# Cross attention of a decoder layer: score terms of a head pair stacked by DMA into one product of 100 rows, all engines' work in a group in a new order, and two implied waits left out

## The chip, the cores and the metric

The kernel runs on one core of one Trainium2 chip. The metric is the device time of one execution in microseconds (us). TensorE (PE) multiplies, VectorE (DVE), ScalarE (ACT) and GpSimd (POOL) compute elementwise, SyncE (SP) issues most DMAs. Each engine works through its own instructions in their order and waits on semaphores.

## The reference

Four sequences of 1024 tokens, width 256, 77 context rows each. Three blocks are added to x in turn, each behind a layer norm: a recurrent block (shift, projections, a scan), cross attention over the context, and a mixture of 16 experts (top 2).

```python
x = x + attn(layernorm(x))                 # scan over time, 64 states
q = (layernorm(x) @ wq.T + bq)             # 16 heads of 16
k, v = ctx @ wk.T + bk, ctx @ wv.T + bv    # 77 keys
x = x + softmax(q k^T / 4) v @ wo.T + bo
x = x + moe(layernorm(x))                  # top 2 of 16 experts, 256 wide, gated
```

## The kernel before

The work has three stages. The first does the recurrent block for all 4096 tokens, then `s1_turn`. The second is the cross attention with the router of the experts, in 8 groups of 512 tokens (`GROUPS`; two groups share a sequence b). The third, the experts, takes 79 blocks of 128 rows that the router has scattered to `xs_rows` in memory.

A group passes through three phases that run one group apart. Phase 1 of group g+1: norm by ScalarE (`norm_q`, L685), turn by TensorE (`s1_turn`, L970) and copy (`evac_t`, L696), query products (`s1_q`, L977), the fp16 high half QH by ScalarE (`evac_q`, L703) and the low half QL by VectorE (`s1_ql`, L1386), then an estimate of each head's score maximum: 16 products `s1_max` (L985) into two banks, each reduced by VectorE (L1396), negated into high and low halves (`s1_mh`, L1400), turned (`s1_mt`, L1000) and copied to MT (`evac_m`, L709). Phase 2 of group g: for each half m of the heads (8 heads), 616 key columns in 5 chunks of 128 (the last 104). `s2_scores` (L1006) adds four products into a bank: minus the maxima over an indicator matrix IND (32 rows), then high keys by low queries, low keys by high queries and high by high, where the keys stand block by block, masked per head, in KCUR (`kcur`, L495, by POOL). Two banks alternate; ScalarE takes the exponential of each chunk into PB (`exps`, L715). Then `s2_pv` (L1026) makes numerator and denominator in fp32, by products of 32 columns each, with VCUR (`vcur`, L1271, by VectorE from memory) and a mask MV. `s2_attn` (L1408) divides. PB, NUM and DEN are single, so the exponentials of one half wait for the value product of the other. Phase 2 of group g-1 ends with the out projection (`s2_out`, L1046), the residual add (`s2_x2`, L1414) and the norm before the experts (`root3`, `norm_3`, `rows_hi`, `low_rows`, `s3_turn`). Phase 3 of group g-2: logits (`s3_logits`), top 2, prefix sums (`s3_prefix`, L1072), slots (`s3_slots`, L1465) and 8 scatters by POOL (L542). The banks of the logits and prefix sums are those of the maxima, so the maximum products wait for the run counts (`run_s`).

The order within a group is written out by hand in a function `body` for each engine (TensorE's at L1078, ScalarE's at L750, VectorE's at L1491, POOL's at L553), called in a loop over b for the middle groups. In TensorE's body: 5 chunks of m=0, logits, out projection, turn, prefix, value product m=0, query products, 5 chunks of m=1 with the 16 maximum products between their products, value product m=1, turn of the maxima, `s3_turn`. Beside this the 48 pieces of expert weights are loaded by SP (`wload`, L320), scaled and rounded by ScalarE (`whi`, L613) and their low halves made by POOL (`split`, L487): 6 pieces before the groups, 6 in each of the first 7 groups. At the end POOL scatters the last group, SP and ScalarE write padding rows (`pads`, L300), and TensorE starts the experts' products when all 48 pieces are split (L1138).

## Time and profile before

| | us |
|---|---|
| median of 3 runs (769.19 to 773.58) | 772.86 |
| the profiled execution | 767.49 |
| its span, first to last instruction | 765.7 |
| TensorE, VectorE, POOL, ScalarE busy | 613.7, 488.7, 351.0, 328.9 |
| mean granted TensorE clock | 0.898 |

"Busy" is the time in which at least one instruction of that engine runs. A granted clock of 1.00 is 2.4 GHz and of 0.50 is 1.2 GHz. In rows of the timeline the columns are start, length, engine, line, operation, output and inputs, number of instructions merged, and in brackets the idle time before and what ended it.

### The profile page before, as it was taken

The page shows a single profiled execution, that of the slowest core. Times are in us where ns is not written, and L with a number is a line of the kernel's source. Part 1 is how long each engine was busy: PE and PEld are TensorE (multiplying, and loading weights), DVE is VectorE, ACT ScalarE, POOL GpSimd, SP SyncE. Part 2 cuts the span into 40 slices and gives each one's busy share as a digit, 9 for nine tenths or more (in the row PEclk, how much of TensorE's full clock was granted, in tenths as well). Part 3 has the DMA queues.
Part 4 walks back from the last instruction along what each step waited for, and adds up shares of the span by engine and source line. Part 5 has one row for each costly group of instructions (what it writes and reads, how often), then busy time and mean ns, then how long its engine had stood idle before and what let it go on. Part 6 is the DMA issues. An engine that isn't in the chain of part 4 may idle for free.

```text
span 765.7 us, 13490 instructions
## 1 busy us (share of the span) xinstructions
PE 613.7 (80%) x3148; PEld 314.6 (41%) x3149; DVE 488.7 (64%) x1381; ACT 328.9 (43%) x739; POOL 351.0 (46%) x433
## 2 busy tenths in 40 slices
PE   1987888778999797979798973069999999999910
PEld 0666333523434252525252543034555555555510
DVE  5576325756487566866767644446777777777796
ACT  3854634226666464655555332013333333333331
POOL 5864623232744656467557355412333333333353
PEclk9998987679999899989899985579999999999975
DMA  9811000074000101010101011523333333333397
GB/s 321 272 11 12 0 1 0 2 270 146 1 1 12 49 2 56 4 55 0 55 1 57 1 55 56 168 55 84 91 87 88 85 87 88 86 86 88 73 377 275
DMA packets 93219, 62.37 MB, mean 81 GB/s; under 512 B 68186, under 2 KB 78558, under 8 KB 93056
## 3 DMA queue, kind: packets, MB, share of 16 engines
q1 hardware_dynamic: 85168, 44.04, 20.8%
q0 software_dynamic: 6864, 16.86, 6.5%
q10 hardware_dynamic: 1152, 1.06, 0.5%
q8 instruction: 15, 0.25, 0.1%
q14 instruction: 20, 0.16, 0.1%
HBM read 27.97 MB, written 25.56 MB: 70 GB/s over the span
## 4 chain that ended last, share of the span: by engine, by line
PE 51%; SPq 14%; DVE 12%; issue 9%; ACT 6%; DMA 4%; POOL 2%; another core or an unknown queue 1%; ACTq 0%; POOLq 0%; DVEq 0%
SPq L379 7%; PE bank L1037 5%; PE bank L891 4%; PE bank L866 4%; PE bank L995 3%; PE bank L1017 3%; SPq L380 3%; PE bank L855 3%; PE bank L1054 3%; PE bank L1019 3%; SPq L375 3%; PE bank L1068 2%; PE bank L1160 2%; PE bank L1161 2%; PE bank L1163 2%
## 5 line engine op out<-in xcount | busy, mean ns | idle before, releaser
L588 POOL DMA_INDIRECT y_rows<-AR x79 | 77.2, 977 | 165.4 <-ACT AR L815 161.1
L491 POOL TENSOR_TENSOR W<-STG,W 128x512 f16<-128x512 f32 (+1 forms) x48 | 56.1, 1169 | 122.2 <-ACT W L620 120.9
L804 ACT ACTIVATE AR<-AR 128x256 f32<-128x256 f32 x79 | 32.9, 417 | 160.4 <-DVE AR L1585 138.1
L1410 DVE RECIPROCAL AR<-bank 128x512 f32<-128x512 f32 x16 | 53.7, 3354 | 38.1 <-PE bank L1037 31.2
L548 POOL DMA_INDIRECT xs_rows<-AR,SLOT x64 | 63.4, 991 | 27.4 <-issue 18.1
L720 ACT ACTIVATE AR<-bank 128x512 f32<-128x512 f32 (+1 forms) x80 | 47.6, 596 | 51.9 <-PE bank L1023 47.9
L1396 DVE TENSOR_REDUCE MX<-bank 128x4 f32<-128x308 f32 x128 | 56.6, 475 | 18.4 <-PE bank L995 13.8
L1585 DVE TENSOR_SCALAR AR<-bank 128x256 f32<-128x256 f32 x79 | 33.5, 424 | 51.5 <-PE bank L1163 47.9
L1160 PE MATMUL bank<-W,AR 128*128 x158 | 61.3, 388 | 0.0
L1161 PE MATMUL bank<-W,AR 128*128 x158 | 61.1, 387 | 0.0
L995 PE MATMUL bank<-KCUR,AR 128*128 (+1 forms) x128 | 41.9, 329 | 19.4 <-DVE MX L1396 10.0
L1601 DVE TENSOR_TENSOR AR<-bank,AR 128x256 f16<-128x256 f32 x79 | 33.5, 425 | 24.1 <-ACT AR L808 20.2
L1163 PE MATMUL bank<-W,AR 128*128 x158 | 47.9, 385 | 0.0
L1158 PE MATMUL bank<-BEX,AR 128*128 128x512 f16 x79 | 30.9, 391 | 20.2 <-DMA AR<-xs_rows 18.2
L1181 PE MATMUL bank<-W,AR 128*128 x158 | 40.7, 277 | 0.0
L1182 PE MATMUL bank<-W,AR 128*128 x158 | 40.6, 277 | 0.0
L1037 PE MATMUL bank<-AR,VCUR 128*32 128x512 f32 (+1 forms) x256 | 35.8, 682 | 4.3 <-ACT AR L720 4.3
L815 ACT ACTIVATE AR<-bank 128x256 f32<-128x256 f32 x79 | 30.1, 381 | 15.5 <-PE bank L1184 13.5
L1172 PE MATMUL bank<-ID,AR 128*128 128x128 f32 x158 | 32.3, 286 | 4.8 <-issue 2.8
L1596 DVE SCALAR_TENSOR_TENSOR AR<-AR 128x256 f32<-128x256 f32 x79 | 33.6, 425 | 2.7
L995 PEld LDWEIGHTS bank<-KCUR,AR 128*128 128x128 f16 x128 | 12.4, 98 | 52.6 <-DVE MX L1396 28.8
L620 ACT ACTIVATE W<-STG 128x512 f16<-128x512 f32 (+1 forms) x48 | 30.2, 630 | 8.2 <-ACT STG L618 5.0
(229 smaller groups left out, 1443.6 us busy)
## 6 DMA issues: line engine op xcount, KB each, us to landing
W<-in_wexp SPq DMA_DIRECT2D x16, 768.0 KB, 5.3
W<-y_rows SPq DMA_DIRECT2D x8, 1024.0 KB, 15.3
X<-in_x SPq DMA_DIRECT2D x4, 1024.0 KB, 11.9
out<-X SPq DMA_DIRECT2D x8, 512.0 KB, 8.1
CST<-in_cst SPq DMA_DIRECT2D x1, 1309.0 KB, 8.4
AR<-xs_rows SPq DMA_TRANSPOSE x79
AR<-xs_rows SPq DMA_DIRECT2D x79, 1.0 KB
y_rows<-AR POOLq DMA_INDIRECT x79
```

What stands on the lines that cost most here:

```text
L379: sp.dma_start_transpose(XTS[:, q], xs_halves[ds(row, P), 0:2 * D]).then_inc(XTIN[q], 16)
L491: pool.tensor_tensor(w[:, 1], STG[:, q], w[:, 0], ALU.subtract).then_inc(s["w_split"], 1)
L548: pool.indirect_dma_start(xs_rows, bass.IndirectOffsetOnAxis(ap=SLOT[:, par, k, j:j + 1], axis=0), RB[:, par, j, :], None, bounds_check=XS ...
L588: pool.indirect_dma_start(y_rows, bass.IndirectOffsetOnAxis(ap=NIX[:, k:k + 1], axis=0), CY[:, k, :], None, bounds_check=TOPK * NTOK - 1, ...
L720: act.activation(PB[0:rows, c, :], SC[(m * NCH + c) % 2][0:rows, :], ACT.Exp)\
L995: pe.matmul(MXB[:, half, 0:GK // 2], QH[:, par, m, j * P:(j + 1) * P], KCUR[:, ds(bp, 1), m, 0, 4 * half:4 * half + 4].rearrange("p a h k ...
L1037: mm = pe.matmul(o[32 * j:32 * j + 32, :], w[0:rows, j + v, v].rearrange("p a e -> p (a e)"), PB[0:rows, j + v, :], start=(v == 0), stop=( ...
L1160: pe.matmul(GUP[q], XTS[:, k, c], w_at(e, c * 2 * PW + LOW, F), start=False, stop=False)
L1161: pe.matmul(GUP[q], XTS[:, k, c], w_at(e, c * 2 * PW, F), start=False, stop=False)
L1163: mm = pe.matmul(GUP[q], XTS[:, k, 2 + c], w_at(e, c * 2 * PW, F), start=False, stop=(c == DC - 1))
L1396: dve.tensor_reduce(MX[:, j, m * HG + 4 * half:m * HG + 4 * half + 4], MXB[:, half, 0:GK // 2].rearrange("p (h k) -> p h k", k=KEYS), AX.X ...
L1410: dve.reciprocal(AT[:, m], DEN[:, :]).then_inc(s["rec_s"], 1)
```

## The change

**Keys and queries.** For each pair of heads, KS holds a block of 100 rows: high, low and again high halves of 32 rows of keys, and 4 rows of a pattern of ones that picks the minus maxima of its heads. QS holds the matching rows of the queries: high, high, low, and four rows of maxima. One product over 100 rows gives the sum of all four terms. Four chunks of an m are now 64 keys of two heads (128 columns); the fifth holds the other 13 keys of all eight heads, each pair in 32 columns, by four narrow products. QS is filled in every group through memory: QH and QL are written to `q_rows` and read back in 6 DMAs, MT is written to `m_rows` and read back in 2, all issued by SP (`q_stack`). QH and QL are single now, so `evac_q` waits for their writes. KS is filled once, before the first group, from masked copies KM that POOL makes. KCUR keeps only the high half. V is copied once into VP and VR, so `vcur` and the trip through `v_flat` go, as does IND.

**Order.** All four bodies are rewritten, TensorE's loop over groups is written out, and the pieces of weights are now 12 before the groups, 3 in each of the 8, 6 before the last scatter and 6 behind it; the last two experts are loaded after all value products.

**Two waits.** `c_gu` no longer waits for `cu_r`, nor `c_tg` for `cgl_r`; both are implied by other waits.

```diff
@@ SP, once @@
+            sp.wait_ge(s["km_r"], 1)
+            kv_in(KS[3 * 32:QROWS].rearrange("p n b k -> p (n b) k"),
+                  PAT[3 * 32:QROWS].unsqueeze(1).broadcast_to([QROWS - 3 * 32, PAIRS * B, PKW]))
+            for m in range(DC):
+                for i in range(GT):
+                    for t, v in enumerate((0, 1, 0)):
+                        kv_in(KS[32 * t:32 * t + 32, m * GT + i].rearrange("p b k -> p (b k)"),
+                              KM[32 * i:32 * i + 32, v, m].rearrange("p b k -> p (b k)"))
...
@@ SP, each group @@
+            def q_stack(g):
+                first = g == 0
                 for m in range(DC):
+                    sp.wait_ge(s["ql_r"], 2 * g + (m + 1))
+                    if not first:
+                        sp.wait_ge(QSIN[m], g * QS_IN)
+                    for v, q in enumerate((QH, QL)):
+                        sp.dma_start(q_rows[m, v], q[:, m]).then_inc(QOUT[m], 16)
                 for m in range(DC):
+                    sp.wait_ge(QOUT[m], 32 * g + 32)
+                    if not first:
+                        sp.wait_ge(s["sc_mm"], g * (2 * NCH) - (1 - m) * NCH)
+                    for t, v in enumerate((0, 0, 1)):
+                        sp.dma_start(QS[32 * t:32 * t + 32, m], q_in[m, v]).then_inc(QSIN[m], 16)
+                sp.wait_ge(s["mT_r"], g + 1)
+                sp.dma_start(m_rows, MT[:, :]).then_inc(s["m_out"], 16)
+                sp.wait_ge(s["m_out"], 16 * g + 16)
+                for m in range(DC):
+                    sp.dma_start(QS[3 * 32:QROWS, m], m_in[m]).then_inc(QSIN[m], 16)
+            for g in range(GROUPS):
+                q_stack(g)
+                wload(g + (A_EXP + 2))
@@ POOL @@
+            for n in range(A_PIECES // 2):
+                split(n, n % 2)
+            pool.wait_ge(s["a_kv"], 4)
+            pool.memset(CST[:, 0:B * DC * P], 0.0).then_inc(s["vr_z"], 1)
+            for n in range(A_PIECES // 2, A_PIECES):
                 split(n, n % 2)
...
             def body(g, b, par, out=True, log=True, attn=True, nxt=True, nextk=None):
                 if attn:
+                    for k in range(PIECES):
+                        split(g * PIECES + (A_PIECES + k), (par + k) % 2)
                     add_bo(g)
...
+            for n in range(B_PIECES, C_HALF):
+                split(n, n % 2)
             scatter(GROUPS - 1, 1)
+            for n in range(C_HALF, NPIECE):
+                split(n, n % 2)
@@ ScalarE body @@
                 if attn:
+                    for k in range(PIECES):
+                        whi(g * PIECES + (A_PIECES + k), (par + k) % 2, g * 16 + 16 * (A_EXP + 1))
+                if nxt:
+                    for j in range(GT):
+                        norm_q(g + 1, j)
+                if attn:
+                    exps(g, 0, 0, first)
+                    exps(g, 0, 1, first)
                 if log:
                     pair_exp(g - 2)
...
                 if nxt:
                     evac_t(g + 1)
...
+                if attn:
+                    exps(g, 0, 2, first)
+                if nxt:
+                    evac_q(g + 1, 0)
+                if attn:
+                    exps(g, 0, 3, first)
+                if nxt:
+                    evac_q(g + 1, 1)
+                if attn:
+                    exps(g, 0, 4, first)
                 if out:
                     norm_3(g - 1)
                     rows_hi(g - 1, 1 - par, b - 1 + par)
@@ TensorE @@
+                o = SC[(m * NCH + c) % 2]
+                if c < GT:
+                    mm = pe.matmul(o[:, :], KS[0:QROWS, m * GT + c, b, 0:P], QS[0:QROWS, m, c], start=True, stop=True)
+                else:
+                    for i in range(GT):
+                        mm = pe.matmul(o[32 * i:32 * i + 32, :], KS[0:QROWS, m * GT + i, b, P:PKW],
+                                       QS[0:QROWS, m, i], start=True, stop=True)
+                mm.then_inc(s["sc_mm"], 1)
...
                 if out:
                     s2_out(g - 1)
+                if attn:
+                    s2_scores(g, b, 0, 0)
+                    s2_scores(g, b, 0, 1)
                 if nxt:
                     s1_turn(g + 1)
+                if attn:
+                    s2_scores(g, b, 0, 2)
+                if nxt:
+                    s1_q(g + 1, 0)
+                if attn:
+                    s2_scores(g, b, 0, 3)
+                if nxt:
+                    s1_q(g + 1, 1)
+                if attn:
+                    s2_scores(g, b, 0, 4)
                 if log:
                     s3_prefix(g - 2)
...
                     units = s1_max(g + 1, 1 - par, b1, bp1) if nxt else iter(())
+                    for _ in range(2):
+                        next(units, None)
+                    s2_pv(g, b, 0, units)
                     for c in range(NCH):
+                        s2_scores(g, b, 1, c)
+                        for _ in range(1):
+                            next(units, None)
                     s2_pv(g, b, 1, units)
+                    for _ in units:
+                        pass
...
-                if not isinstance(n, int) or n >= 2:
-                    pe.wait_ge(s["cu_r"], n - 1)
                 pe.wait_ge(XTIN[k], 16 * (t + 1))
...
                 pe.wait_ge(s["cgd_r"], n + 1)
-                if not isinstance(n, int) or n >= 2:
-                    pe.wait_ge(s["cgl_r"], n - 1)
@@ VectorE body @@
                 if log:
                     s3_slots(g - 2, par)
+                if nxt:
+                    s1_ql(g + 1, 1 - par)
+                    s1_max(g + 1, 0, 5)
                 if attn:
                     s2_attn(g, 0)
                 if nxt:
-                    s1_ql(g + 1, 1 - par)
-                    s1_max(g + 1)
+                    s1_max(g + 1, 5, 16)
                     s1_mh(g + 1)
```

In `s2_pv` a maximum product is taken after each quarter but the last: three in each value product.

## Rows read from the trace of the kernel before

**Rows 1.** Windows by stage: length; busy PE, PEld, DVE, ACT, POOL; clock, DMA, GB/s.

```profile
147.00:503.00 356.00, 282.66 (x1461) 127.12 (x1460) 221.28 (x614) 169.32 (x328) 185.50 (x224) 0.88 0.17 54
503.00:731.00 228.00, 217.32 (x1253) 120.62 (x1253) 162.89 (x474) 80.10 (x235) 74.64 (x77) 0.98 0.37 88
```

**Rows 2.** The same view, one group of the loops.

```profile
359.90:400.10 40.20, 35.25 (x189) 15.38 (x187) 27.13 (x73) 22.69 (x45) 22.13 (x27) 0.92 0.08 27
```

**Rows 3.** Timeline of TensorE: starts of value products of groups 1, 2, 6, 7.

```profile
206.42 1.06 PE L1037 MATMUL bank<-AR,VCUR 128*32 128x512 f32 x8
222.66 0.64 PE L1037 MATMUL bank<-AR,VCUR 128*32 128x512 f32 x4 [0.52 <-ACT AR L720]
240.44 1.06 PE L1037 MATMUL bank<-AR,VCUR 128*32 128x512 f32 x8
...
400.07 1.50 PE L1037 MATMUL bank<-AR,VCUR 128*32 128x512 f32 x12
433.30 1.93 PE L1037 MATMUL bank<-AR,VCUR 128*32 128x512 f32 x16
```

**Rows 4.** Timeline, TensorE: a score chunk's first and last product, and the next chunk's first.

```profile
347.14 0.38 PE L1017 MATMUL bank<-MT,IND 32*128 32x512 f16 x1
...
347.90 0.38 PE L1023 MATMUL bank<-AR,KCUR 128*128 128x512 f16 x1
...
348.21 0.38 PE L1017 MATMUL bank<-MT,IND 32*128 32x512 f16 x1
```

**Rows 5.** Timeline, all engines, 352 to 370 us, group 5.

```profile
352.45 1.85 PE L1068 MATMUL bank<-CST,AR 128*128 128x16 f32 x16
354.16 3.71 PE L1054 MATMUL bank<-CST,AR 128*128 128x256 f32 x16
358.86 1.09 PE L967 MATMUL bank<-ID,AR 128*128 128x128 f32 x8 [0.99 <-DVE X L1420]
359.93 1.93 PE L1037 MATMUL bank<-AR,VCUR 128*32 128x512 f32 x16
360.33 1.07 ACT L699 ACTIVATE AR<-bank 128x512 f32<-128x512 f32 x2
361.67 1.91 PE L1037 MATMUL bank<-AR,MV 128*32 128x512 f32 x16
362.43 0.78 DVE L1475 TENSOR_TENSOR RUN<-RUN,bank 128x16 f32<-128x16 f32 x4
363.51 3.70 PE L981 MATMUL bank<-AR,CST 128*128 128x512 f32 x8
368.54 1.41 DVE L1389 SCALAR_TENSOR_TENSOR AR<-bank,CST,AR 128x512 f16<-128x512 f32 x2
```

**Rows 6.** Windows around the end of a group's scatters, columns as in rows 1.

```profile
374.00:377.00 3.00, 0.62 (x3) 0.11 (x2) 0.76 (x2) 0.83 (x2) 2.30 (x3) 1.00 0.25 88
377.90:384.30 6.40, 5.89 (x24) 1.75 (x27) 2.52 (x7) 2.39 (x5) 3.07 (x4) 0.50 0.00 0
```

**Rows 7.** Timeline of SP's queue: V written to memory, and the first read back.

```profile
54.07 4.04 SPq L335 DMA_DIRECT2D v_flat<-W  x8
60.75 0.40 SPq L346 DMA_DIRECT2D VFLAT<-v_flat  x1
```

**Rows 8.** The page's part 5: groups with busy time, mean ns, idle time before.

```profile
L1410 DVE RECIPROCAL AR<-bank 128x512 f32<-128x512 f32 x16 | 53.7, 3354 | 38.1 <-PE bank L1037 31.2
L720 ACT ACTIVATE AR<-bank 128x512 f32<-128x512 f32 (+1 forms) x80 | 47.6, 596 | 51.9 <-PE bank L1023 47.9
L1396 DVE TENSOR_REDUCE MX<-bank 128x4 f32<-128x308 f32 x128 | 56.6, 475 | 18.4 <-PE bank L995 13.8
```

**Rows 9.** Timeline: the last two early pieces, the first query norm, the first expert product.

```profile
129.01 2.44 POOL L491 TENSOR_TENSOR W<-STG,W 128x512 f16<-128x512 f32 x2 [0.41 <-ACT W L620]
139.71 2.07 ACT L692 ACTIVATE AR<-X,RSQ 128x256 f32<-128x256 f32 x4 [5.06 <-POOL RSQ L439]
502.92 0.61 PE L1158 MATMUL bank<-BEX,AR 128*128 128x512 f16 x1 [15.29 <-DMA AR<-xs_rows]
```

More of the change, by code:

```diff
@@ L362, in _ @@
+            for g in range(GROUPS):
+                q_stack(g)
+                wload(g + (A_EXP + 2))
+            sp.wait_ge(s["pv_mm"], 2 * GROUPS)
+            for e in range(A_EXP + 2 + GROUPS, NEXP):
+                wload(e)
             sp.wait_ge(s["c_tab"], 1)
@@ L554, in body @@
                 if attn:
+                    for k in range(PIECES):
+                        split(g * PIECES + (A_PIECES + k), (par + k) % 2)
                     add_bo(g)
-                if attn and nxt:
-                    for k in range(PIECES):
-                        split(g * (2 * PIECES) + (A_PIECES + k), k % 2)
                 if out:
@@ L562, in body @@
                     scatter(g - 2, par)
-                if attn and nxt:
-                    for k in range(PIECES, 2 * PIECES):
-                        split(g * (2 * PIECES) + (A_PIECES + k), k % 2)
                 if out:
@@ L799, in _ @@
             pair_exp(GROUPS - 1)
+            for n in range(B_PIECES, C_HALF):
+                whi(n, n % 2, 16 * (n // PIECES + 1))
             def c_tanh(n, q):
@@ L819, in _ @@
             pads(act, 1)
+            for n in range(C_HALF, NPIECE):
+                whi(n, n % 2, 16 * (n // PIECES + 1))
             c_tanh(0, 0)
@@ L1116, in _ @@
             s1_mt(0)
[L1117 to L1123 removed]
+            for g in range(GROUPS):
+                n = (g + 1) // 2
+                body(g, g // 2, g % 2, g // 2 % 2, n, n % 2, out=g >= 1, log=g >= 2, nxt=g + 1 < GROUPS)
             body(GROUPS, None, 0, None, None, None, attn=False, nxt=False)
```

328 lines of the change are left out of this document (150 added, 178 removed).

## The prediction, as it was put on record

> **What bounds the kernel now.** I read the stages first [rows 1]. The experts' stage is TensorE at its own pace, 217 of 228 us busy. The attention stage holds TensorE busy 283 of 356 us, and the change works there. So the question is what sets the length of one group of 512 tokens in it. The window over one group of the loops [rows 2] has TensorE at 35 of 40 us and no other engine over 28, which looks like a TensorE bound. The timeline says otherwise. I take the start of the first value product (m=0; `s2_pv` at L1037) as the mark of a group. Group 5's is at 359.93, group 6's at 400.07 [rows 3, 5]: 40.1 us. The undisturbed time is seen earlier: 206.42 to 222.66 (m=0 to m=1, 16.2 us) and 222.66 to 240.44 (m=1 to the next m=0, 17.8 us), so 34.0 us [rows 3]. The other 6 us, less a fraction for the router's work that group 1 has not, come with the eight scatters of a group: near the last one TensorE is busy 0.62 of 3 us while VectorE and ScalarE also wait, and then the granted clock is 0.50, the level of 1.2 GHz, for 6.4 us [rows 6]. I take this disturbance as 5.3 us a group. What the profile calls a TensorE-bound group is a chain that goes around four engines, most links of which are not score products.
>
> **The change, part by part.** *Score products.* Five chunks for each m, of four products each, are now one product of 100 rows each, and for the fifth chunk four narrow ones side by side. A chunk takes 1.07 us from start to start [rows 4], so ten take 10.7; a product takes 0.22 by the middle three starts. The narrow value products show that four of 32 columns run at once: eight fp32 ones, the first half of `s2_pv`, take 1.74 us by their start to the second half's [rows 5], against 0.92 for one wide fp32 product (four in 3.70). So ten chunks cost about 2.4 us, and 8.3 us of TensorE's 35 go. The extra spacing of 0.31 instead of 0.22 in front of the 32-row product [rows 4] goes too; but each maximum product between value products now changes width twice, and I charge 0.3 us for each of six. The Trainium skill (TensorEngine Tiling, Key Properties) says that a change of tiling mode drains TensorE; by that rule these six cost their changes; the trace agrees as far as 0.1 us a change. If only their own 0.13 counted, a group would be 1.0 shorter and the sum 8 less.
>
> *Order.* What counts is the chain. I follow it in an undisturbed group of the new order from the end of the value product m=0 (0 us), with durations from [rows 5] and, for an exponential (0.60 us), the reciprocal (3.35) and a maximum (0.47), from [rows 8].
> (a) VectorE now does five of the sixteen maxima, then `s2_attn` m=0 (reciprocal and product, 4.1 us), then the rest. TensorE's seventh maximum product onwards is queued in order between the score chunks and waits for maximum 6, at 4.7. Behind it stand chunks 3 and 4 of m=1, then the last exponential: m=1's value product starts at 6.7. In the kernel before this stretch was 12.8 us (16.2 less the product itself), so 6 us are won.
> (b) Value product 3.5 with three maximum products in it: 11.2. The last three maxima with their two-bank exchange, and the negation: 13.4.
> (c) Transposes of the maxima, the router's turn 1.1, its copy 1.1 by ScalarE: 15.7. Logits 1.8, out projection 3.6: 21.2 (the second reciprocal is done at 17.5, hidden). Before, chunks of m=0 stood here and hid the copy.
> (d) Residual add 0.7, turn 1.1: 23.2. The copy of the turn comes after two exponentials: 24.8.
> (e) The query products, 3.7 in two halves with chunks 2 and 3, now stand *before* the value product m=0 and not behind it: 28.9.
> (f) The last chunk and `s3_prefix`, which has moved behind the query products: 29.7. VectorE has waited for it since about 24.7, and behind that wait (`s3_slots`) are queued the low half of the queries and all maxima. Run counts 1.1 us, in which the maximum products may not start: value product m=0 from 31.2.
> (g) Inside it the third maximum product waits for the first maximum: slots 1.0, low halves 1.4, maximum 0.45: 33.8. Then three quarters of the value product and three maximum products: 37.0.
> So an undisturbed group takes 37.0 against 34.0 to 34.6 us. TensorE's saving is real and ends in waits. With the same disturbance of 5.3 it is 42.3 against 39.9 (the mean of the four intervals from 240.44 to 400.07).
> Is the disturbance the same? The slots come at 31.9, eight scatters of 1.28 us follow, and the last ends near 5 us after the next value product: just where maxima, chunk 3 and exponentials alternate. It is on the path again. TensorE is sparse from 0 to 6.7 also without it, and in a group without scatter I add 1.5 us for the clock.
>
> *Stacking by DMA.* Per group SP issues 4 writes and 6 reads of 128 KB, the maxima out and in (3 small ones), and one 768 KB weight load. The queries' part is ready by about 44 and needed at 58, so it is hidden by the end of the value product and all of phase (a) to (c). The maxima leave at 14.5 and chunk 0 is wanted at 21.2. A write to memory and its wait cost 0.5 to issue (eight in 4.04) and 2.6 to land [rows 7]; no row shows a small read, so I take between 2.2 and 2.7 with its issue, up to 1 more for the second issue: 5.7 to 6.8 us, just hidden by 6.7. If it is late, the out projection is already past and chunk 0, the turn and all behind it slip by the excess. Only in group 0 is it bare: +6.1. The Trainium skill (DMA: Bandwidth & Descriptors, Anatomy of one DMA) gives a fixed 2.0 us a transfer on another issuing path; by it the trip would be about 5 and hidden with room, while the measured 2.6 is slower.
>
> *Head.* Six more weight pieces are split before the first queries' roots. The six of before began on ScalarE at 121.38 and ended on POOL at 131.45 [rows 9], 10.1 us. The new ones start behind the last tanh/exp pair at 134.65, end at 144.7, and POOL's two roots of 2.6 us follow: the first query norm is at 150.0 and not 139.71 [rows 9]. VectorE's adds held TensorE until 146.8, so 4.4 us of the 10.3 show. With the trip: +10.5. POOL's pattern of indicators (10 us) goes and head masks of about the same size come, hidden by the wait before the first splits. The 35 small copies for keys and values (SP, 0.5 each, 18 us) end well before 153.
>
> *First groups.* Between the first chunk and the end of value product 0 the turn and the query products of group 1 now intervene, at 1.2 GHz (2.1 and 5.3), so 15 us where it was 11.5: +3.5. Group 0 to 1, where neither router nor scatter is: phases (a) to (e) as above, then the low half and the first maximum at once, 34.0 and 1.5 for the clock against 32.9: +2.6. Group 1 to 2, no scatter: 38.5 against 34.0, +4.5. Groups 2 to 6, four intervals at 2.4: +9.6. Group 7: neither turn nor queries, even in the first half, and m=1's scores save 2.6.
>
> *Experts' entry.* Six pieces are split before the last scatter, and six behind. POOL is free 3 us before that and a piece takes about 1.3, so the scatter starts 5 us later and takes 10.2; ScalarE issues its eight pads behind its pieces and splits the rest after them. The first expert product waits for all 48 pieces. It stood at 502.92 [rows 9] behind pads, their landing and a transposing load; with the pieces it is 4 later (2 to 9).
>
> *Two waits dropped.* They were implied, so no data wait goes; the only gain is TensorE's queue. In this stage TensorE is idle for 11 us in all [rows 1], part of it for the data of the gate, so the bounds are 0 and 11, and I take 2.
>
> **Sum.** 10.5 + 3.5 + 2.6 + 4.5 + 9.6 - 2.6 + 4 - 2 = +30 us. The profiled execution took 767.5, the median of the runs is 772.9; I carry the difference over: 803 us.
>
> **Rivals.** *TensorE was the bound* (faster). If VectorE and ScalarE run ahead, so that waits (f) and (g) are met on arrival, a group loses its 8.3 us: 31.6. Eight groups give -66, with 12.5 for head, entry and the dropped waits: 719. It needs `s3_prefix` to be off the path, and it decides from where a group is under 38.3 us (12.5/8 below 39.9). For it: TensorE's 35 of 40. Against it: the ordered waits above. Chance 0.13.
> *No disturbance* (about even). If the bare straight-line program of TensorE, or the shifted scatter, avoids the 5.3 us in five groups and the 1.5 in two: 803 - 29.5 = 774. The unrolled group 6 had less of it, 400.07 to 433.30 only 33.2 us [rows 3], against me; but it had no turn behind. Chance 0.12.
> *Sparse TensorE* (slower still). The clock falls also around the query products and (g), or the maxima's trip is late by 1: 1.5 to 3.5 more a group, +12 to +28: 823. For it: the clock fell after three sparse microseconds [rows 6], and (a), (d) and (g) are as sparse. Chance 0.17.
> *The narrow products don't run side by side*: 0.66 more for each of 16 chunks, +10, inside my range. Chance 0.03.
> *My forecast*: 0.55.
>
> **Range and chances.** 0.5% is 3.9 us, about what a measurement of this kernel can tell from no change. The forecast's own range is 785 to 820; with the even and the sparse case it becomes 770 to 830. Under 769: most of the TensorE case and a little of the even one, 0.17. Within: 0.08. Above 777: 0.75.
>
> **What would show it.** Right: the mark's interval near 42 us in groups 2 to 6; TensorE busy near 26 of it; the wait for the first maximum inside value product m=0; VectorE idle in front of the run counts; the first chunk of group 0 near 176; the first expert product 4 us behind what the shift of the router's end gives. Wrong: an interval under 38, chunk 0 waiting for the QS transfers in the loop groups, or the third maximum product starting with no idle time before it.

## The result, and the profile of the changed kernel

The changed kernel takes 809.2 us (median, 806.4 to 811.2) beside 771.0 us (768.9 to 773.6) for the kernel before on the same chip: a ratio of 1.049, 95% interval 1.044 to 1.054. The profiled execution took 806.42 us with a span of 804.7, and the one of before 767.49 with 765.7, so 39.0 us of span are to be found.

The page of the changed kernel, its parts 2 (granted clock in tenths, 40 slices) and 5 (line, operation, count, busy and mean ns, idle before). TensorE's busy time is 594.5 us (74%); it was 613.7 (80%).

The first line is the clock row of the kernel before, the second that of the changed kernel; the last two lines are the output projection, before (from the view of groups by line) and changed.

```profile
PEclk9998987679999899989899985579999999999975
...
PEclk9998987558887888797969688558999999999965
...
L1459 DVE TENSOR_REDUCE MX<-bank 128x4 f32<-128x308 f32 x128 | 58.3, 475 | 54.3 <-PE bank L1071 50.1
...
L1071 PE MATMUL bank<-KCUR,AR 128*128 128x308 f16 x128 | 41.4, 345 | 41.0 <-DVE MX L1459 27.3
...
L1054 PE MATMUL bank<-CST,AR 128*128 128x256 f32 x128 | 31.9, 405 | 0.0
...
L1125 PE MATMUL bank<-CST,AR 128*128 128x256 f32 x128 | 45.4, 531 | 4.5 <-DVE AR L1475 4.5
```

The score products' time is gone, yet VectorE now waits 54.3 us for maximum products where it waited 18.4 [rows 8], and a record of the output projection (L1125) takes 531 ns on average, where it took 405. (The trace records each fp32 product twice, so 16 records are eight products.) The clock rows show why: in the attention stage, slices 8 to 28 of the 40, a 9 stands three times; it stood twelve times.

The windows of one group, as in [rows 2] (length; busy PE, PEld, DVE, ACT, POOL; clock, DMA, GB/s): first group 5 to 6 with router and scatter, then group 1 to 2, which has neither.

```profile
391.30:433.30 42.00, 31.52 (x163) 14.47 (x166) 26.48 (x68) 18.57 (x38) 17.92 (x23) 0.84 0.24 77
223.50:264.30 40.80, 32.69 (x158) 15.52 (x158) 25.27 (x64) 19.32 (x39) 10.01 (x15) 0.79 0.16 48
```

The mark of a group, the start of value product m=0, stands at 186.61, 223.48, 264.36, 306.66, 350.15, 391.26, 433.25 and 471.80 us. The timeline of TensorE in group 5 answers to [rows 3 to 6]; the numbers in brackets are idle time ahead of a row and what ended it.

```profile
391.26 1.06 PE L1108 MATMUL bank<-AR,W 128*32 128x512 f32 x8
393.64 0.30 PE L1071 MATMUL bank<-KCUR,AR 128*128 128x308 f16 x1 [1.31 <-DVE MX L1459]
...
399.23 0.39 PE L1092 MATMUL bank<-W,KS 100*128 100x512 f16 x1 [1.01 <-issue]
403.03 0.44 PE L1071 MATMUL bank<-KCUR,AR 128*128 128x308 f16 x1 [3.42 <-issue]
...
405.40 1.94 PE L1108 MATMUL bank<-AR,W 128*32 128x512 f32 x8 [0.33 <-ACT AR L788]
...
413.86 0.40 PE L1079 MATMUL bank<-ID,MH 128*32 128x128 f16 x4 [1.08 <-DVE MH L1467]
414.19 1.09 PE L1043 MATMUL bank<-ID,AR 128*128 128x128 f32 x8
416.02 3.60 PE L1139 MATMUL bank<-CST,AR 128*128 128x16 f32 x16 [0.74 <-ACT AR L810]
419.45 5.12 PE L1125 MATMUL bank<-CST,AR 128*128 128x256 f32 x16
424.42 0.60 PE L1092 MATMUL bank<-W,KS 100*128 100x512 f16 x2
...
427.33 1.98 PE L1057 MATMUL bank<-AR,CST 128*128 128x512 f32 x4 [0.52 <-ACT AR L767]
...
431.18 0.40 PE L1095 MATMUL bank<-W,KS 100*32 100x512 f16 x4
...
432.88 0.44 PE L1071 MATMUL bank<-KCUR,AR 128*128 128x308 f16 x2 [1.14 <-DVE LG L1542]
433.25 1.06 PE L1108 MATMUL bank<-AR,W 128*32 128x512 f32 x8
```

VectorE beside it (the reciprocal of m=0 and the maxima behind it, then the run counts), and TensorE's same hole in group 1:

```profile
398.51 3.36 DVE L1473 RECIPROCAL AR<-bank 128x512 f32<-128x512 f32 x1 [1.58 <-PE bank L1112]
402.50 0.86 DVE L1459 TENSOR_REDUCE MX<-bank 128x4 f32<-128x308 f32 x2
...
431.78 0.79 DVE L1538 TENSOR_TENSOR RUN<-RUN,bank 128x16 f32<-128x16 f32 x4 [3.68 <-PE bank L1147]
...
232.85 0.44 PE L1071 MATMUL bank<-KCUR,AR 128*128 128x308 f16 x1 [3.19 <-DVE MX L1459]
```

Three things are to be seen. The third maximum product waits inside the value product (1.31). The eighth (403.03) waits 3.42 us, because VectorE has put the reciprocal of m=0 between its maxima; this hole is in group 1 too, 3.19 us, where nothing is scattered. And the clock is low twice: in m=1's value product (1.94 for the first four products, which are eight records; 1.06 at full clock) and again through logits and output projection, 3.60 and 5.12 us where [rows 5] have 1.85 and 3.71.

Where the 39.0 us are, by the marks of the two traces:

| stretch | before | changed | more | forecast |
|---|---|---|---|---|
| up to the first score chunk | 165.45 | 174.94 | +9.5 | +10.5 |
| to mark 0 | 8.1 | 11.7 | +3.6 | +3.5 |
| mark 0 to 1 | 32.9 | 36.9 | +4.0 | +2.6 |
| mark 1 to 2 | 34.0 | 40.9 | +6.9 | +4.5 |
| mark 2 to 6, four intervals | 159.6 | 168.9 | +9.3 | +9.6 |
| mark 6 to 7 | 33.2 | 38.6 | +5.3 | 0 |
| mark 7 to the first expert product | 69.6 | 73.0 | +3.4 | +1.4 |
| experts to the end | 262.8 | 259.9 | -2.9 | -2 |

### The profile page after: what moved, and what is told of

The parts are those of the page before. It is cut to its first block, busy times and chain, and to the rows that moved or that the text cites. A ratio compares the mean times of both kernels' runs of the same rounds, so it can differ in the third digit from the quotient of the medians.

```text
span 804.7 us, 12825 instructions
## 1 busy us (share of the span) xinstructions
PE 594.5 (74%) x2956; PEld 307.0 (38%) x2957; DVE 493.5 (61%) x1365; ACT 327.6 (41%) x739; POOL 337.7 (42%) x438
## 3 DMA queue, kind: packets, MB, share of 16 engines
q10 hardware_dynamic: 1152, 1.06, 0.5%
## 4 chain that ended last, share of the span: by engine, by line
PE 40%; SPq 16%; DVE 16%; issue 11%; ACT 6%; DMA 5%; POOL 4%; another core or an unknown queue 1%; DVEq 0%; ACTq 0%; POOLq 0%
SPq L424 8%; PE bank L1125 4%; PE bank L1057 4%; PE bank L1112 4%; PE bank L1108 4%; PE bank L942 4%; PE bank L967 4%; SPq L425 3%; SPq L420 3%; PE bank L1071 3%; PE bank L931 3%; DVE AR L1473 2%; PE bank L1139 2%; DVE MX L1459 2%; DMA AR<-xs_rows 2%
## 5 line engine op out<-in xcount | busy, mean ns | idle before, releaser
L1459 DVE TENSOR_REDUCE MX<-bank 128x4 f32<-128x308 f32 x128 | 58.3, 475 | 54.3 <-PE bank L1071 50.1
L878 ACT ACTIVATE AR<-AR 128x256 f32<-128x256 f32 x79 | 32.9, 417 | 133.2 <-DVE AR L1646 110.0
L788 ACT ACTIVATE AR<-bank 128x512 f32<-128x512 f32 x80 | 45.9, 594 | 78.5 <-PE bank L1092 51.2
L1071 PE MATMUL bank<-KCUR,AR 128*128 128x308 f16 x128 | 41.4, 345 | 41.0 <-DVE MX L1459 27.3
L1473 DVE RECIPROCAL AR<-bank 128x512 f32<-128x512 f32 x16 | 53.7, 3355 | 17.9 <-PE bank L1112 13.1
L1125 PE MATMUL bank<-CST,AR 128*128 128x256 f32 x128 | 45.4, 531 | 4.5 <-DVE AR L1475 4.5
L1257 PE MATMUL bank<-W,AR 128*128 x158 | 40.9, 278 | 0.0
L1125 PEld LDWEIGHTS bank<-CST,AR 128*128 128x128 f32 x128 | 35.2, 282 | 12.2 <-DVE AR L1475 4.8
L1057 PE MATMUL bank<-AR,CST 128*128 128x512 f32 x64 | 35.3, 682 | 4.2 <-ACT AR L767 4.2
L684 ACT ACTIVATE STG<-W 128x512 f32<-128x512 f32 (+1 forms) x48 | 29.8, 621 | 19.9 <-issue 11.9
L1092 PE MATMUL bank<-W,KS 100*128 100x512 f16 x64 | 25.3, 422 | 15.6 <-ACT AR L788 6.1
```

The lines of the kernel that those rows point to most:

```text
L1057: mm = pe.matmul(WK[m][:, :], CST[:, C_WQ + c * D + m * P:C_WQ + c * D + (m + 1) * P], XQT[:, c, :], start=(c == 0), stop=(c == DC - 1))
L1071: pe.matmul(MXB[:, half, 0:GK // 2], QH[:, m, j * P:(j + 1) * P], KCUR[:, bp, m, 4 * half:4 * half + 4].rearrange("p h k -> p (h k)"), sta ...
L1125: mm = pe.matmul(WK[j // 2][:, (j % 2) * D:(j % 2 + 1) * D], AT[:, c, j * P:(j + 1) * P], cst_w(C_WO, D, c), start=(c == 0), stop=(c == DC ...
L1459: dve.tensor_reduce(MX[:, j, m * HG + 4 * half:m * HG + 4 * half + 4], MXB[:, half, 0:GK // 2].rearrange("p (h k) -> p h k", k=KEYS), AX.X ...
L1473: dve.reciprocal(AT[:, m], DEN[:, :]).then_inc(s["rec_s"], 1)
```

## Experiments

The reading to be tested was: the new order's chain sets the group, and stacking itself saves time. The rivals: TensorE's load was the bound, or TensorE's low clock is what costs. "Interval" is the mean distance of the marks from group 2 to 6 in the profiled execution (before 39.9, changed 42.2 us). The run below that moves the last pieces leaves these groups alone and has 42.6: so well does an interval repeat. Diffs are shortened, and in part put in words.

**The old order with stacked scores.** On TensorE (ScalarE and VectorE likewise: exponentials of m=0 together, evacuation of the queries behind the router's rows, `s2_attn` of m=0 ahead of all maxima):

```diff
-                s2_scores 0, 1; s1_turn; s2_scores 2; s1_q(g + 1, 0); s2_scores 3; s1_q(g + 1, 1); s2_scores 4
-                s3_prefix; two maxima; s2_pv(g, b, 0, units); then one maximum behind each chunk of m=1
+                s2_scores 0 to 4; s1_turn; s3_prefix; s2_pv(g, b, 0)
+                s1_q(g + 1, 0); s1_q(g + 1, 1); then two maxima behind each chunk of m=1
```

> The changed kernel with one thing put back: on TensorE, ScalarE and VectorE the order inside a group is again that of the kernel before (five score chunks, turn, prefix, value product m=0, then the query products and the sixteen maximum products), with the logits and the output projection still ahead of the first chunk. The stacked scores, the DMA trips and the piece split stay. Theory (the chain of the new order sets the group: query products ahead of value product m=0, a third maximum that waits for the first, VectorE waiting for the prefix behind chunk 4): value product m=0 starts some 5 us after the residual add instead of 9, and the mark interval of groups 2 to 6 falls from 42.2 to 37 or 38, so the kernel gets 25 to 35 us faster than the changed one: 775 to 785. Rival (the order doesn't matter, sparse TensorE with its lower clock or VectorE's own work sets the group): the interval stays within 1 us of 42, and the time within 5 us of 809.

Measured: 770.2 us (768.2 to 772.6), ratio 1.001 (0.998 to 1.003), interval 37.5. This is the kernel's whole loss: with the stacked products, their transfers and the new piece split in place and only the order put back, the time is that of before. The theory holds, with 5 us more gained than the 775 expected, and the rival by which the order doesn't matter falls. The same stretches as above in this run's group 5:

```profile
360.31 1.07 PE L1101 MATMUL bank<-AR,W 128*32 128x512 f32 x8
...
363.88 3.70 PE L1050 MATMUL bank<-AR,CST 128*128 128x512 f32 x8
...
375.03 1.93 PE L1101 MATMUL bank<-AR,W 128*32 128x512 f32 x8 [1.72 <-issue]
...
386.11 3.56 PE L1132 MATMUL bank<-CST,AR 128*128 128x16 f32 x16 [0.74 <-ACT AR L810]
389.50 5.43 PE L1118 MATMUL bank<-CST,AR 128*128 128x256 f32 x16
394.77 0.60 PE L1085 MATMUL bank<-W,KS 100*128 100x512 f16 x2
...
398.33 1.06 PE L1101 MATMUL bank<-AR,W 128*32 128x512 f32 x8
```

From the end of the projection to the mark, which is the start of value product m=0, it is 3.6 us (394.77 to 398.33), and 8.8 in the changed kernel (424.42 to 433.25). Value product m=0 takes 3.6 us up to the query products, and 6.1 with three maxima and a wait in it (391.26 to 397.34). In exchange the new order has only 27.1 us from there to the end of the projection, where this one has 30.9. So moving the query products ahead costs 5.3 and 2.5, and wins 3.8: they took 3.7 us behind value product m=0, but the maxima are no quicker without them there, since they wait for VectorE. The run puts three engines' orders back at once; these parts are read from one group of two timelines and weren't timed one by one. Also to be seen: logits and projection are slow here too, 3.56 and 5.43.

**The old load in both orders.** Every score product issued four times to the same place, which gives TensorE 7.2 us a group back.

```diff
+                for _ in range(3):
+                    (the chunk's product, or its four narrow ones, once more)
                 if c < GT:
                     mm = pe.matmul(o[:, :], KS[0:QROWS, m * GT + c, b, 0:P], QS[0:QROWS, m, c], ...)
```

> The changed kernel with every score product issued four times to the same place (the last one counts), which gives TensorE back about the score work of the kernel before: some 2.4 us more three times, 7 us more in a group. It is the new order with the old load. Theory (chunks and query products in one row on TensorE between the residual add and value product m=0 are on the path): the five chunks of m=0 add about 3.7 us per group, those of m=1 stand beside VectorE's maxima and add 0 to 3; interval 42 to 46 to 48, time 840 to 850. Rival (the clock is what costs in the new order): the granted clock in the output projection comes back to 1.00, which gives back about 3.4 us per group, and the interval stays near 42 to 44, time 810 to 825.

> The old order of all engines' work and every stacked score product issued four times: old order, old load, with the DMA trips and the new piece split. Theory: the interval is that of the kernel before, 39 to 41, and the time is that of before plus the head's +9.5, the experts' entry +4 and the later stage's -3, so 780 to 787. The distance to the old order with single products tells what TensorE's 8 us per group are worth in the order for which they were on the path: 2 to 4 us per group by the theory, 8 by the rival that TensorE alone was the bound.

| interval, time, ratio | one product | four |
|---|---|---|
| old order | 37.47, 770.2, 1.001 | 40.23, 794.1, 1.032 |
| new order | 42.22, 809.2, 1.049 | 46.36, 826.6, 1.075 |

Of 7.2 us put on TensorE 2.8 come out in the old order and 4.1 in the new. So TensorE was never the bound for all of its work, and stacking is worth 2.8 to 4.1 a group; the new order costs 4.8 to 6.1. The new order's interval, 46.4, is as expected, but its time of 827 lies between the two ranges, below the 840 of the theory and above the 825 of the clock rival. The old order's interval with the old load, 40.2, is that of before. Its time came out at 794 and not at 780 to 787: mark 0 stands 8.2 us later than before (181.75), the time from mark 2 to mark 6 is the same within 1.3, and the first expert product comes at 531.85, 28.9 later. Half of that arose in groups 0 to 2 and behind mark 6 (417.6 to 457.6 there, 40.1 us; before 33.2), which I had counted as even; why the kernel before is so quick from mark 6 to 7 is not settled. The clock stays low in projection and logits of this last run (546 and 361 ns a record), so more score work behind them doesn't bring it back.

**The prefix alone moved ahead.**

```diff
                 if nxt:
                     s1_turn(g + 1)
+                if log:
+                    s3_prefix(g - 2)
                 ...
                     s2_scores(g, b, 0, 4)
-                if log:
-                    s3_prefix(g - 2)
```

> The changed kernel with one thing moved: the two prefix products stand right behind the turn of the queries, ahead of chunk 2, instead of behind chunk 4. VectorE then counts the runs while TensorE is in the query products, and the low halves and the first maximum don't wait for it. Theory (term g of the sum, the wait inside value product m=0): the third maximum comes 2 to 2.5 us earlier, idle ahead of the run counts falls from 3.7 to under 1, interval 42.2 to about 40, time 793 to 800. Rival (the next wait, VectorE's maxima or ScalarE, is as late): under 0.5 us per group, 805 to 811.

Measured: 810.5 us, ratio 1.055 (1.048 to 1.062), interval 43.3. The expectation of a gain was wrong, and the rival holds. The local step did as said; TensorE, group 5:

```profile
393.76 0.30 PE L1071 MATMUL bank<-KCUR,AR 128*128 128x308 f16 x1
...
400.55 0.44 PE L1071 MATMUL bank<-KCUR,AR 128*128 128x308 f16 x1 [2.36 <-issue]
403.51 0.61 PE L1092 MATMUL bank<-W,KS 100*128 100x512 f16 x1 [2.52 <-ACT AR L788]
406.68 0.44 PE L1071 MATMUL bank<-KCUR,AR 128*128 128x308 f16 x1 [2.56 <-DVE MX L1459]
```

The third maximum starts with no idle ahead of it, 1.0 us behind the mark and not 2.4. But where the changed kernel has one hole of 3.4 us, this one has three, 7.4 us in all. The scatter starts 1.3 us ahead of the mark (391.42) and not 1.5 behind it (392.74), and its stall, in which VectorE waits too, no longer falls into the hole of the reciprocal but lies in front of it. From value product m=0 to m=1 it is 15.6 us in groups 2 to 6, and 14.5 in the changed kernel. The clock is lower too: its mean from mark 2 to mark 6 is 0.79, and 0.84 in the changed kernel. That the shifted stall is the cause in each group is read from one timeline and not tested.

**Trip to memory lengthened.** The maxima are written twice, one write behind the other, ahead of the load.

```diff
-                sp.dma_start(m_rows, MT[:, :]).then_inc(s["m_out"], 16)
-                sp.wait_ge(s["m_out"], 16 * g + 16)
+                for r in range(2):
+                    sp.dma_start(m_rows, MT[:, :]).then_inc(s["m_out"], 16)
+                    sp.wait_ge(s["m_out"], 32 * g + 16 * (r + 1))
```

> The changed kernel with the maxima written to memory twice, one behind the other, ahead of the load, which lengthens the trip by one write (about 1.3 us by the 1.2 us wait in the trace, some 3.5 us for write and load). Theory (the trip is hidden behind logits and output projection in groups 1 to 7, where the load is issued 7 us ahead of chunk 0, and open in group 0 alone): group 0's first chunk 1.2 to 2 us later, marks of the other groups as far apart as before, time +1 to +2, 809 to 812. Rival (the trip is late in the loop too, beside weight loads and scatters): +1.3 in each group, 818 to 821.

Measured: 805.7 us, ratio 1.047 (1.039 to 1.055), interval 42.5: no difference from the changed kernel. In group 0, the changed kernel and then this one:

```profile
174.94 1.03 PE L1092 MATMUL bank<-W,KS 100*128 100x512 f16 x2 [4.15 <-DMA W<-m_rows]
```

```profile
176.79 1.04 PE L1093 MATMUL bank<-W,KS 100*128 100x512 f16 x2 [5.57 <-DMA W<-m_rows]
```

The wait grows by 1.4 us there and nowhere else. The transfers are hidden in the loop.

**Last pieces moved.** Six behind the exponentials of group 7, six ahead of the last scatter.

```diff
+            for n in range(B_PIECES, C_HALF): whi(n, ...)     (ahead of the last body, ScalarE and GpSimd)
             body(GROUPS, ...)
             ...
+            for n in range(C_HALF, NPIECE): whi(n, ...)       (ahead of the pads and the last scatter)
```

> The changed kernel with its last twelve weight pieces moved: six go behind the last exponential of group 7, where ScalarE and GpSimd are idle, and six ahead of the last scatter instead of behind it. Nothing stands between the pads and the transposing loads then. Theory (the entry to the experts costs about 4 us because TensorE waits for six pieces behind ScalarE's pads): the first expert product comes when its loads have landed, 3 to 6 us earlier, time 803 to 806. Rival (loads, scatter and pads end as late without them): within 1 us of the changed kernel.

Measured: 805.9 us, ratio 1.046 (1.039 to 1.054); against the changed kernel's 1.049 that is no difference that can be told (the range expected was 803 to 806). From mark 7 to the first expert product it is 68.9 us and not 73.0:

```profile
541.90 0.61 PE L1236 MATMUL bank<-BEX,AR 128*128 128x512 f16 x1 [13.91 <-DMA AR<-xs_rows]
```

The releaser is the transposing load now, so the six pieces had held TensorE. What they cost isn't settled: two other runs keep the changed kernel's code in this stretch (the prefix moved, the trip lengthened), and it takes 71.8 and 70.3 us in them. So the move wins between 1.4 and 4.1 us. From here to the end it takes 263.2 us, 259.9 in the changed kernel, and 260.7 and 262.3 in those two; whether a part is given back there can't be told from that.

**Only the two waits dropped, in the kernel before.**

```diff
-                    pe.wait_ge(s["cu_r"], n - 1)
...
-                    pe.wait_ge(s["cgl_r"], n - 1)
```

> The kernel before with the two implied waits of the experts' stage taken out, and nothing else. Theory (-2 in the sum, since each wait is met before TensorE asks for it and costs only its own instruction): 0 to 3 us faster, 767 to 771, and the same from the first expert product to the end within 3 us. Rival (the waits hold TensorE back at each tile): over 5 us faster, up to 11.

Measured: 767.6 us, ratio 1.000 (0.996 to 1.004); experts' stage 261.9 us against 262.8. The waits cost nothing that can be measured. The changed kernel's 259.9 is the shortest of three profiles of that code (260.7 and 262.3 in the runs with the prefix moved and the trip lengthened), so how much of the -2.9 in the table above is real isn't settled.

**Scores ahead of the logits again.** The trace of the old order says that the clock is lost at two waits in front of the logits. In the kernel before, the chunks of m=0 filled them.

```diff
+                s2_scores(g, b, 0, c)  for all c, ahead of s3_logits and s2_out
-                        for _ in range(2): next(units, None)
-                    s2_pv(g, b, 1, units)
+                        for _ in range(4 if c else 0): next(units, None)
+                    s2_pv(g, b, 1, turn_max(g + 1))            (s1_mt behind its second quarter)
+                piece(g, par, k)                                (pieces behind the exponentials)
```

> The old order with stacked scores, and beside it what the trace of that run asks for: the maxima of the next group are done in value product m=1's wait and not behind it (four maximum products behind each of chunks 1 to 4), their transposes stand inside value product m=1, so that the trip to memory runs behind the second half of it, and the five score chunks of m=0 stand ahead of the logits again, where they fill the wait for the router's evacuation; the three weight pieces of a group move behind ScalarE's exponentials. Theory (what the stacked order loses over the old one is that logits and output projection run at 1.2 GHz behind two TensorE waits, 3.6 and 5.4 us instead of 1.9 and 3.7, and that the tail of the maxima stands behind value product m=1): interval 37.5 to 32 to 35, the projection back at 3.7 us, time 745 to 760, faster than both. Rival (the trip to memory, 3.5 us, now ends late ahead of chunk 0 and takes the gain back, or VectorE's maxima push value product m=1 back as far): interval 36 to 38, time 765 to 775.

Measured: 794.8 us, ratio 1.032 (1.024 to 1.040), interval 41.0. My theory fell. Of the rival the late trip is seen, but the loss is far larger than its 36 to 38:

```profile
404.57 1.09 PE L1040 MATMUL bank<-ID,AR 128*128 128x128 f32 x8
407.00 0.60 PE L1094 MATMUL bank<-W,KS 100*128 100x512 f16 x2 [1.34 <-DMA W<-m_rows]
...
410.03 0.62 PE L1097 MATMUL bank<-W,KS 100*32 100x512 f16 x4 [0.36 <-ACT AR L789]
410.57 3.60 PE L1141 MATMUL bank<-CST,AR 128*128 128x16 f32 x16
```

TensorE waits for the maxima from memory, then the five chunks take 3.6 us, 1.4 of them waiting for ScalarE, and the clock falls all the same. A run further down (maxima and their transposes ahead) moves the maxima in the same way, but keeps the chunks behind the projection and the pieces where they were: 34.2. So the chunks ahead of the logits and the moved pieces cost 6.8 us a group together; no run parts the two. As the rows have it, a stacked score chunk is too short to fill the wait, and it needs its trip: it belongs behind the logits and the projection, where the change put it.

**Extra products in the waits.** In the old order, sixteen products a group whose result isn't used.

```diff
+                    fill(8)      (eight of ID16 x KRAW, 308 columns, into the free score bank)
                     s1_mt(g + 1)
 ...
+                        fill(8)
                     s3_logits(g - 2)
```

> The old order with stacked scores, and sixteen extra products a group (fp16, 308 columns, their result isn't used) in two of TensorE's waits: eight ahead of the transposes of the maxima (idle 1.1 us there) and eight ahead of the logits (idle 0.7 us). They cost some 0.13 us each at 2.4 GHz, 2.1 us a group, of which 1.8 lie in the waits. Theory (in the stacked kernels the granted clock falls to 1.2 GHz for logits and projection because TensorE has holes in front of them, which the score products filled in the kernel before): the clock stays at 2.4 GHz there, logits 1.9 instead of 3.6, projection 3.7 instead of 5.4, interval 37.5 to about 34.5, time 750 to 758. Rival (the fall there has another cause, the long stall near the end of the scatter or the load since then): the clock falls all the same, the products cost 0 to 2 us a group, 770 to 782.

Measured: 757.7 us, ratio 0.983 (0.977 to 0.990), interval 35.5.

```profile
379.76 0.40 PE L1072 MATMUL bank<-ID,MH 128*32 128x128 f16 x4
380.09 1.09 PE L1036 MATMUL bank<-ID,AR 128*128 128x128 f32 x8
381.02 1.21 PE L1078 MATMUL bank<-KRAW,ID 128*128 128x308 f16 x8
382.06 1.85 PE L1137 MATMUL bank<-CST,AR 128*128 128x16 f32 x16
383.77 3.71 PE L1123 MATMUL bank<-CST,AR 128*128 128x256 f32 x16
```

Logits and projection are back at 1.85 and 3.71 us, and 2.0 of the 3 us expected come out; the mean clock from mark 2 to mark 6 is 0.88, and 0.84 without the products. Work that is of no use makes this kernel faster, because it closes the holes in front of the work that is: here the clock's part is shown apart from the order. Which of the two holes counts the run doesn't tell. The Trainium skill (TensorE: Matmul & The Clock Gate, HAM oscillation — how this bites in real kernels) describes a kernel whose wait in each round makes the clock fall in each round; by that rule the holes cost more than their length, and this run agrees: 2.1 us of extra products, put mostly into 1.8 us of holes, win 2.0. The page's waits are longer ones, for data; that holes of 1.1 and 0.7 us can bring the clock down is what the run adds.

**Maxima and their transposes ahead**, first alone and then with the extra products. The diff is the middle part of the one for scores first; logits and projection stay ahead of the chunks.

> The old order with stacked scores, logits and projection ahead of the chunks as in that run, and one thing moved: all sixteen maximum products stand behind the score chunks 1 to 4 of m=1, and the transposes of the maxima inside value product m=1. By the traces of the two old-order runs value product m=1 then starts 17.3 instead of 14.7 us behind value product m=0 and ends at 22.4 instead of 22; the router's turn ends 1.6 us earlier, and the reciprocal of m=1 starts 1 us earlier. Theory: interval 37.5 to 36 to 36.5, time 762 to 767. Rival (the maxima at the end of value product m=1 were hidden; value product m=1 later by 2.6 us is what counts): interval 37.5 to 39, 770 to 780.

> Both: maxima and their transposes ahead, and eight extra products (fp16, 308 columns, result not used) ahead of the logits. Theory: if the clock can be held, logits and projection take 1.9 and 3.7 us, and the interval is 33 to 34.5, time 742 to 755, clearly faster than the kernel before. Rival: the clock falls all the same and the eight products stand in the wait for the router's evacuation, so the time is that of the run without them, within 3 us.

> The last of the three again, with four more extra products ahead of the output projection, where TensorE waits 0.5 us for VectorE's reciprocal. In the run without them the logits are at 2.4 GHz (1.85 us) and the projection at 1.2 GHz (5.4 us). Theory (the fall takes the hole nearest to it): projection 3.7 us, interval 35.0 to 33.3, time 745 to 752. Rival (the engine has been too little at work over a longer stretch, and a few products at the last wait change nothing): projection 5.2 to 5.4 us, interval within 0.7 us of 35, time 756 to 762.

| run | time | ratio | interval | projection, group 5 |
|---|---|---|---|---|
| maxima and turns ahead | 756.4 | 0.983 (0.978 to 0.987) | 34.2 | 5.27 |
| and 8 ahead of the logits | 761.6 | 0.987 (0.979 to 0.994) | 35.0 | 5.41 |
| and 4 ahead of the projection | 760.3 | 0.983 (0.977 to 0.989) | 34.9 | 3.73 |

The first is better than I had expected, 34.2 for 36 to 36.5, and it is the shortest interval of all. Every group of it from 2 to 6 has 16.5 us to m=1 and 17.4 to 17.9 from there. The extra products do nothing on top: with eight the clock fell again in the projection; with twelve it held in the projection of every group, but then TensorE waited 0.52 us for VectorE's residual add, and from m=0 to m=1 it took 17.4 us on average instead of 16.5, so the interval stayed. The low clock had in part only moved. The windows of the four groups in the run with twelve:

```profile
251.03:284.87 33.84, 29.16 (x174) 14.07 (x171) 27.57 (x61) 18.65 (x38) 20.45 (x25) 0.95 0.29 97
284.87:319.29 34.42, 30.24 (x174) 13.91 (x171) 26.38 (x74) 18.49 (x38) 17.98 (x24) 0.85 0.29 94
319.29:353.62 34.33, 29.46 (x174) 13.99 (x171) 27.47 (x62) 18.85 (x39) 20.31 (x25) 0.94 0.29 94
353.62:390.63 37.01, 32.03 (x172) 14.42 (x170) 26.88 (x67) 18.63 (x37) 17.97 (x23) 0.82 0.28 88
```

Two groups have a clock near full; the last is the longest and has the lowest, and there value product m=0 itself began at 1.2 GHz. Without extra products each of these groups has 0.85. The theory was right on the projection's clock and wrong on the time. The three are not told apart by their intervals. All are faster than both kernels, than the one before by 1.3 to 1.7%; the first has stacked scores, the old order and a few moved products, and no extra work.

## Why the prediction came out as it did

The forecast was 803 us in a range of 770 to 830; it came out at 809. The direction and the main mechanism, the new order's chain, were the forecast's. That the interval came out within 0.1 us was luck: the sum had the clock too small and the disturbance too large, by at least 4 us each. By its steps:

- **Head**, +10.5 for +9.5. The first query norm stands at 150.00, as forecast, and TensorE's first turn 4.5 us later. The trip was mis-sized: from the end of the maxima's copy, 171.47, to chunk 0 at 174.94 it is 3.5 us and not 6.1. The write is seen as landed 1.5 us behind the start of its issue, where I had taken 3.1 (0.5 and 2.6) from a queue of eight larger ones [rows 7]; the read takes 2.0 more. SP's queue in the changed kernel:

```profile
171.49 0.32 SPq L394 DMA_DIRECT2D m_rows<-MT  x1
172.97 0.59 SPq L397 DMA_DIRECT2D W<-m_rows  x2
```

  That 1.6 us more came between turn and transposes was not forecast.
- **(a)** The eighth maximum product (the forecast counted the seventh) waits for VectorE behind `s2_attn`, with chunks 3 and 4 behind it; shown by the hole of 3.4 us. Value product m=1 starts 7.0 us behind the end of m=0's in group 1 (6.7 forecast). That the hole brings the clock down I had charged with 1.5 a group without scatter only, and here the reckoning failed.
- **(b), (c)** In group 1 the transposes come 15.3 us behind (13.4), the projection ends 27.4 behind (21.2). Nearly all of the difference is the clock: the first four value products at 1.94 us, logits 3.59 for 1.8, projection 6.69 for 3.6. The second fall, in logits and projection, stood nowhere in the sum, and costs 4.7 us here and some 3.2 in group 5.
- **(d), (e), (f)** Confirmed: query products ahead, then the prefix, then VectorE idle for 3.68 us in front of the run counts, then 1.1 us of counts. The old-order run shows that this is what loses: 5.3 us between projection and mark.
- **(g)** Confirmed, 1.3 us of wait. But moving the prefix, which takes this wait and VectorE's wait in (f) away, gains nothing. The move shifts the scatter as well, so what either wait costs by itself isn't shown.
- **Disturbance.** The term of 5.3 us a group was wrong for the new order. Group 1 to 2, with no scatter, takes 40.9 us, and the loop groups 42.2, so scatter and router add 1.3. In group 5 value product m=1 starts 2.4 us later behind the mark than in group 1 (14.1, 11.7), by the wait of (g) and 1.0 us more of VectorE's wait ahead of the reciprocal; from there to the next mark it is 1.3 us shorter (27.8, 29.1), with the projection at 5.12 instead of 6.69. The last scatter lies beside the reciprocal's hole, which hardly grows (3.42, 3.19), and the clock falls behind it in both groups. The forecast's 37.0 + 5.3 and the trace's 40.9 + 1.3 meet at 42.3 and 42.2: two errors of at least 4 us cancelled in groups 2 to 6 (of more, since 37.0 holds the wait of (g) and group 1's 40.9 doesn't), and don't in 0 to 2 (+3.8 missed together) and in 6 to 7.
- **Group 7.** "Even in the first half" missed 5.3 us: group 6's interval has the maxima, the hole and both low clocks in it; only what follows the mark of group 7 is short.
- **Maximum products inside value products** were charged at 0.3 each. Four value products take 0.86 us from start to start alone and 0.99 with one maximum ahead, and the maximum takes 0.24, so it is 0.37 with both changes of width. Right in kind.
- **Entry** +4: between 1.4 and 4.1 by moving the pieces. **Two waits** -2: not theirs, they cost nothing.
- TensorE busy "near 26 of 42" was 31.5. The low clock stretches it: the mean over the window is 0.84, and the forecast's products were at full clock.
- The rival that TensorE was the bound (719 us) falls by the fourfold products. The rival of sparse TensorE was right that the clock falls a second time, but not on the place: it had the query products, which ran at full clock (1.98 and 1.88 us a half), and it is logits and projection that ran slow. What that adds is what the disturbance doesn't.

What stays open: what in the scatter's last microseconds holds all engines, and whether its stall is what lengthens m=0 to m=1 in the run with twelve extra products. Leaving the scatters out was not tried, since the experts' stage reads what they write.

## What to carry to other kernels

Ask of each wait on TensorE not only how long it is but what stands behind it: behind holes of 1.1 and 0.7 us a fixed piece of fp32 work took 3.4 us longer here, and with useless products in the holes the group was 2.0 us shorter. In another order the same trick brought nothing: try it and time it. A product taken out of a chain that goes around four engines was worth two to three fifths of its time here, and moving other work into the place can lose more than that: change load and order in separate steps and time each. When a sum has an undisturbed part and a disturbance measured elsewhere, look whether the disturbance falls into a hole that the change itself makes.

## What the runs showed of the hardware

- A 32 KB transfer from on-chip memory to HBM was seen as landed 1.5 us behind the start of its issue, and write and read back took 3.5 us (changed kernel, group 0); a second write in a row added 1.4 to the wait.
- TensorE's mean clock was 0.62 while the engine was busy 8.38 of 8.40 us, through logits and projection of the changed kernel's group 5. It stood at 0.50 (1.2 GHz) for the logits and the first 2 us of the projection and rose within the rest; a busy row is no sign of a full clock. The window, columns as above:

```profile
416.00:424.40 8.40, 8.38 (x32) 7.50 (x33) 6.22 (x23) 5.49 (x10) 5.84 (x7) 0.62 0.31 99
```

- Four fp16 products of 100 rows by 32 columns stood side by side: 0.40 us for all four, as long as one of 128 columns (0.39). In the old order's fourfold run twelve of them took 0.66 us from the first's start to the next record, 0.22 for each four, as a product of 128 columns does.
